# Half of an output projection computed as transposed fp32r products of split operands

## What is computed

```
y = y * rsqrt(mean(y*y, axis=-1) + 1e-6)      # 32 heads x 64 channels
y = y * silu(z)
attn = y.reshape(B, T, 2048) @ Wout.T         # (1024, 2048) x (2048, 256)
x = layernorm(x + attn)
```

## Time and profile before

| | |
|---|---|
| median of 3 runs | 721.79 us (719.56 to 722.85) |
| the profiled execution's own time | 723.31 us |
| span of its trace | 721.6 us |
| granted clock, mean over the span | 0.972 |
| PE busy | 658.7 us (91%) |
| PEld / DVE / POOL / ACT busy | 71% / 73% / 64% / 61% |

### The profile page before, as it was taken

One profiled execution on the slowest core, in us unless ns is written; L12 is line 12 of the kernel. 1 busy time (PEld: TensorE's weight loads), 2 busy tenths in 40 slices (PEclk: granted clock), 3 DMA queues, 4 the chain that ended last, 5 costly groups with the idle time before them and its releaser, 6 DMA issues.

```text
span 721.6 us, 11628 instructions
## 1 busy us (share of the span) xinstructions
PE 658.7 (91%) x3388; PEld 510.2 (71%) x3388; DVE 523.5 (73%) x848; ACT 437.3 (61%) x722; POOL 461.6 (64%) x440
## 2 busy tenths in 40 slices
PE   6689999999999999999999999899989998999920
PEld 3467777777777777777777777688867775677710
DVE  4879999999999999999999999613315574222236
ACT  3366797797797797797887887921014544333321
POOL 4066887987887987987888885840025648752034
PEclk9899999999999999999999999999999999999975
DMA  4311211211311211211211200371016914543124
GB/s 148 124 45 59 104 45 59 102 44 58 102 44 58 102 44 58 102 44 58 87 59 58 73 30 0 118 217 36 15 53 147 358 51 106 156 134 97 52 74 131
DMA packets 25475, 62.34 MB, mean 86 GB/s; under 512 B 5206, under 2 KB 18134, under 8 KB 22710
## 3 DMA queue, kind: packets, MB, share of 16 engines
q1 hardware_dynamic: 22278, 53.31, 21.8%
q0 software_dynamic: 3168, 8.67, 4.8%
HBM read 52.77 MB, written 9.20 MB: 86 GB/s over the span
## 4 chain that ended last, share of the span: by engine, by line
PE 83%; DVE 5%; POOL 4%; issue 3%; ACT 2%; DMA 2%; POOLq 0%; SPq 0%; DVEq 0%; ACTq 0%
PE ps L639 35%; PE ps L612 8%; PE ps L653 7%; PE ps L667 6%; PE ps L880 5%; PE ps L920 4%; PE ps L654 4%; DVE conv L1327 3%; POOL conv L577 2%; PE ps L624 2%; PE ps L676 1%; PE ps L768 1%; PE ps L898 1%; PE ps L790 1%; PE ps L872 1%
## 5 line engine op out<-in xcount | busy, mean ns | idle before, releaser
L1327 DVE SCALAR_TENSOR_TENSOR conv<-ps,w_raw,conv 128x506 f32<-128x506 f32 (+3 forms) x352 | 324.9, 935 | 19.9 <-ACT conv L1047 13.7
L639 PE MATMUL ps<-x_hi,w_hi 128*128 128x512 f32 x384 | 166.6, 434 | 9.9 <-DVE conv L1327 8.3
L1047 ACT ACTIVATE conv<-ps,w_raw 128x512 f32<-128x512 f32 x160 | 109.7, 686 | 100.9 <-PE ps L639 99.2
L639 PE MATMUL ps<-x_hi,w_lo 128*128 128x512 f32 x384 | 152.6, 397 | 0.0
L639 PE MATMUL ps<-x_lo,w_hi 128*128 128x512 f32 x384 | 151.9, 396 | 0.0
L404 POOL TENSOR_TENSOR decay<-cum_b,cum_tok 128x512 f32<-128x512 f32 (+1 forms) x128 | 103.2, 827 | 24.6 <-DVE cum_tok L1291 24.6
L639 PEld LDWEIGHTS ps<-x_hi,w_hi 128*128 128x128 f32 x384 | 73.4, 191 | 35.2 <-DVE conv L1327 20.4
L410 POOL TENSOR_TENSOR decay<-decay,mask 128x512 f32<-128x512 f32 x64 | 82.7, 1292 | 5.0
L639 PEld LDWEIGHTS ps<-x_hi,w_lo 128*128 128x128 f32 x384 | 73.0, 190 | 16.8
L639 PEld LDWEIGHTS ps<-x_lo,w_hi 128*128 128x128 f32 x384 | 73.7, 192 | 10.4
L653 PE MATMUL ps<-conv 128*128 128x256 f32 x256 | 78.1, 387 | 2.6 <-DVE xs L1302 1.9
(11 more groups left out here) (219 smaller groups left out, 991.7 us busy)
## 6 DMA issues: line engine op xcount, KB each, us to landing
cum_b<-cum_scratch SPq DMA_DIRECT2D x16, 1024.0 KB, 4.7
w_raw<-in_winT SPq DMA_DIRECT2D x16, 778.0 KB, 4.4
y_all<-in_wgu SPq DMA_DIRECT2D x4, 1408.0 KB, 19.2
ys_scratch<-y_blk SPq DMA_DIRECT2D x31, 128.0 KB, 1.8
late<-in_wdn SPq DMA_DIRECT2D x2, 1408.0 KB
x_scratch<-conv SPq DMA_DIRECT2D x19, 128.0 KB, 6.2
late<-in_woutT SPq DMA_DIRECT2D x1, 2048.0 KB, 8.2
res_scratch<-conv SPq DMA_DIRECT2D x11, 128.0 KB, 1.9
```

The costliest lines, as they stand in the source:

```text
L639: mm = pe.matmul(ps[:, j % 4, :], wp[:, par, w], xp[:, kk, t], start=(i == 0), stop=(i == 5))
L1047: act.activation(conv[:, par, tile, hf * 512:(hf + 1) * 512], ps[:, j % 4, :], ACT.Copy, scale=w_raw[:, par, tap:tap + 1]).then_inc(S["a_c ...
L1327: dve.scalar_tensor_tensor(out=o[:, :, s:], in0=u[:, :, 0:T - s], scalar=w_raw[:, par, c:c + 1], in1=o[:, :, s:], op0=ALU.mult, op1=ALU.ad ...
```

## The change

Blocks 4 to 7 (the last 512 tokens, `HALF`) are no longer computed by `out_project`. `project_half` computes them transposed: stationary is a 128 x 128 piece of the weight, moving are 512 tokens of one pair, the result is 128 outputs x 512 tokens, once for each half c of the 256 outputs (banks 4 and 5). Each product is made of three fp32r ones. So the weight and the half of `y_all` are split first: ACT copies the weight to `wo_hi` in four pieces and each pair to a ring of four buffers, `y_high`; the rests are subtracted by DVE (`wo_lo`, and `y_low` of pairs 0 to 3) and by POOL (`y_low` of pairs 4 to 15, in place of `y_all`). ACT copies the two results to `o_turned`, and PE turns them back with 8 transposes (`turn_half`, banks 6 and 7).

The order of the blocks in the normalization becomes 0, 1, 4, 5, 6, 7, 2, 3. Blocks 2 and 3 stay plain fp32 and come behind `project_half`. The buffers in the former space of `conv` are laid out anew; that moves the load of `ctx_w` and of half of `w_dn` on SP from ahead of the eight stores to behind the second of them, with a wait for the end of `project_half`.

```diff
+HALF = NT // 2
+YRING = 4
+ORDER = (0, 1, 4, 5, 6, 7, 2, 3)
...
@@ sync
-            sp.dma_start(ctx_w, ctxT.rearrange("e (k p) f -> p e k f", p=P)).then_inc(S["ld_ctx"], 16)
...
-            load_down(1)
-            for b in range(TB):
-                sp.wait_ge(S["n0"], b + 1)
+            for pos, b in enumerate(ORDER):
+                if pos == 2:
+                    sp.wait_ge(S["yh_done"], NPAIR)
+                    sp.dma_start(ctx_w, ctxT.rearrange("e (k p) f -> p e k f", p=P)).then_inc(S["ld_ctx"], 16)
+                    load_down(1)
+                sp.wait_ge(S["n0"], pos + 1)
...
@@ gpsimd
+            for i in range(YRING, NPAIR):
+                pool.wait_ge(S["a_yh"], i + 1)
+                t = slice(HALF, NT)
+                pool.tensor_tensor(y_low[:, i, t], y_all[:, i, t], y_high[:, i % YRING, :].bitcast(F32), ALU.subtract
+                                   ).then_inc(S["p_yl"], 1)
             pool.wait_ge(S["v_xin"], 1)
...
@@ tensor
+            def project_half():
+
+                for i in range(NPAIR):
+                    if i % 4 == 0:
+                        pe.wait_ge(S["v_wo"], i // 4 + 1)
+                    if i < YRING:
+                        pe.wait_ge(S["v_yl"], i + 1)
+                    else:
+                        pe.wait_ge(S["p_yl"], i + 1 - YRING)
+                    for c in range(KD):
+                        d = slice(c * P, (c + 1) * P)
+                        for k, (w, y) in enumerate(((wo_hi, y_high[:, i % YRING, :]), (wo_lo, y_high[:, i % YRING, :]),
+                                                    (wo_hi, y_low[:, i, HALF:NT]))):
+                            mm = pe.matmul(ps[:, 4 + c, :], w[:, i, d], y, start=(i == 0 and k == 0),
+                                           stop=(i == NPAIR - 1 and k == 2))
+                    mm.then_inc(S["yh_done"], 1)
+
+            def turn_half():
+
+                for c in range(KD):
+                    pe.wait_ge(S["a_oh"], c + 1)
+                for j in range(2):
+                    for b in (2 * j, 2 * j + 1):
+                        for c in range(KD):
+                            mm = pe.transpose(ps[:, 6 + j, (b % 2) * D + c * P:(b % 2) * D + (c + 1) * P],
+                                              o_turned[:, c, b * P:(b + 1) * P], ident[:, :])
+                    mm.then_inc(S["oh_done"], 1)
...
-            for b in range(TB):
-                if b >= 2:
-                    ge(pe, S["r0"], b - 1)
-                out_project(b, NPAIR - 1 if b < 2 else 0, NPAIR)
...
+            out_project(0, NPAIR - 1, NPAIR)
+            out_project(1, NPAIR - 1, NPAIR)
+            ranks_by_id()
+            project_half()
+            pe.wait_ge(S["r0"], 1)
+            out_project(2, 0, NPAIR // 2)
+            table_by_id()
+            turn_half()
+            out_project(2, NPAIR // 2, NPAIR)
+            pe.wait_ge(S["r0"], 2)
+            out_project(3, 0, NPAIR)
+            pe.wait_ge(S["r0"], 6)
...
@@ scalar
-            for b in range(TB):
-                layer_norm_scale(b, 0)
+            def high_y(i):
+
+                act.wait_ge(S["v_y"], 2 * i + 2)
+                if i >= YRING:
+                    act.wait_ge(S["yh_done"], i - YRING + 1)
+                act.activation(y_high[:, i % YRING, :], y_all[:, i, HALF:NT], ACT.Copy).then_inc(S["a_yh"], 1)
+
+            act.wait_ge(S["ld_wo"], 16)
+            for c in range(4):
+                part = slice(4 * c, 4 * c + 4)
+                act.activation(wo_hi[:, part, :], wo_sb[:, part, :], ACT.Copy).then_inc(S["a_wo"], 1)
+            for i in range(YRING):
+                high_y(i)
+            layer_norm_scale(0, 0)
+            layer_norm_scale(1, 0)
+            for i in range(YRING, NPAIR):
+                high_y(i)
+            act.wait_ge(S["yh_done"], NPAIR)
+            for c in range(KD):
+                act.activation(o_turned[:, c, :], ps[:, 4 + c, :], ACT.Copy).then_inc(S["a_oh"], 1)
+            for pos in range(2, TB):
+                layer_norm_scale(pos, 0)
...
@@ vector
             dve.wait_ge(S["ld_xt"], 16)
-            for b in range(TB):
-                ln_front(b, 0)
-                if b >= 1:
-                    ln_back(b - 1, 0, x1[:, b - 1, :])
...
+            owners_by_id()
+            for c in range(4):
+                dve.wait_ge(S["a_wo"], c + 1)
+                part = slice(4 * c, 4 * c + 4)
+                dve.tensor_tensor(wo_lo[:, part, :], wo_sb[:, part, :], wo_hi[:, part, :].bitcast(F32), ALU.subtract
+                                  ).then_inc(S["v_wo"], 1)
+            for i in range(YRING):
+                dve.wait_ge(S["a_yh"], i + 1)
+                t = slice(HALF, NT)
+                dve.tensor_tensor(y_low[:, i, t], y_all[:, i, t], y_high[:, i, :].bitcast(F32), ALU.subtract
+                                  ).then_inc(S["v_yl"], 1)
+            for n in range(TB):
+                ln_front(n, 0)
+                if n == 1 or n >= 3:
+                    ln_back(n - 1, 0, x1[:, ORDER[n - 1], :])
+                if n == 1:
+                    ln_back(1, 0, x1[:, ORDER[1], :])
                     slots_by_id()
                     tokens_by_id()
...
```

More of the change, by code:

```diff
@@ L83, in build_layer, with shadow @@
         w_raw = sb("w_raw", [P, 2, RAWW])
+        def shadow(name, shape, at):
+            return nc.alloc_sbuf_tensor_at(name, shape, F32R, offset=at)
+        conv_at = -(-nc.sbuf_base // 32) * 32
         conv = sb("conv", [P, 2, NCONV, NT])
@@ L86, in build_layer @@
         xs = sb("xs", [P, TB, P])
+        y_at = -(-nc.sbuf_base // 32) * 32
         y_all = sb("y_all", [P, NPAIR, NT])
@@ L111, in build_layer @@
                                               ("y_lo", [P, 512], F32R)))
+        late_at = -(-nc.sbuf_base // 32) * 32
         late = sb("late", [P, 2, NPAIR * D])
         wo_sb = late[:, 0, :].rearrange("p (i d) -> p i d", i=NPAIR)
+        wo_hi = shadow("wo_hi", [P, NPAIR, D], late_at + 4 * NPAIR * D)
+        wo_lo = shadow("wo_lo", [P, NPAIR, D], conv_at + 4 * YRING * HALF)
+        y_high = shadow("y_high", [P, YRING, HALF], conv_at)
+        y_low = shadow("y_low", [P, NPAIR, NT], y_at)
         xb = sb("xb", [P, NX, D])
@@ L132, in carve @@
             return conv_f[:, at[0] - n:at[0]]
+        xg = carve(TBS * D).rearrange("p (j d) -> p j d", j=TBS)
+        xgT, gT = (carve(2 * KD * P).rearrange("p (r k t) -> p r k t", r=2, k=KD) for _ in range(2))
+        slot_is = conv_f[:, at[0]:at[0] + PICKS * TBS * P // 2].bitcast(BF16).rearrange("p (k t) -> p k t", t=P)
+        ctx_w = carve(EX * KD * D).rearrange("p (e k f) -> p e k f", e=EX, k=KD)
+        at[0] = LATE = YRING * HALF + NPAIR * D
         x_tok = carve(TB * D).rearrange("p (b d) -> p b d", b=TB)
         x1 = carve(TB * D).rearrange("p (b d) -> p b d", b=TB)
[L135 to L142 removed]
+        x2T = conv_f[:, LATE:LATE + KD * TBS * P].rearrange("p (k t) -> p k t", k=KD)
+        res_tok = conv_f[:, LATE:LATE + TB * RES].rearrange("p (b r) -> p b r", b=TB)
+        y_of = conv_f[:, 0:PICKS * TB * D].rearrange("p (k b d) -> p k b d", k=PICKS, b=TB)
+        o_tok = conv_f[:, PICKS * TB * D:LATE].rearrange("p (b d) -> p b d", b=TB)
         g_tok = z_gate[:, 0, 0:2 * D].rearrange("p (r f) -> p r f", r=2)
@@ L183, in build_layer @@
         lane_p = take_c(1)
+        o_turned = take_c(KD * HALF).rearrange("p (c t) -> p c t", c=KD)
         step128 = take_c(TBS)
@@ L218, in build_layer @@
         ld_cum = [sem("ld_cum0"), sem("ld_cum1")]
-        ld_xb = [sem(f"ld_xb{i}") for i in range(NX)]
         st_y = [sem(f"st_y{i}") for i in range(NW)]
         ld_y = [sem(f"ld_y{b}") for b in range(TB)]
-        ld_xg = [sem(f"ld_xg{j}") for j in range(TBS)]
+        ld_row = [sem(f"ld_row{j}") for j in range(max(TBS, NX))]
         block = ctx.enter_context(nc.Block())
@@ L730, in _ @@
             out_project(1, 0, NPAIR - 1)
-            for b in range(TB):
-                if b >= 2:
-                    ge(pe, S["r0"], b - 1)
-                out_project(b, NPAIR - 1 if b < 2 else 0, NPAIR)
-                if b == 2:
-                    ranks_by_id()
-                if b == 6:
-                    table_by_id()
+            out_project(0, NPAIR - 1, NPAIR)
[10 more added lines that the diff above has]
+            pe.wait_ge(S["r0"], 6)
             for _ in range(11):
@@ L1367, in ln_front @@
                 if i == 0:
-                    dve.wait_ge(S["o0"], b + 1)
-                    dve.tensor_tensor(r, ps[:, b % 2, 0:D], x_tok[:, b, :], ALU.add).then_inc(S["r0"], 1)
+                    if 2 <= b < 6:
+                        dve.wait_ge(S["oh_done"], b // 2)
+                        src = ps[:, 5 + b // 2, (b % 2) * D:(b % 2 + 1) * D]
+                    else:
+                        dve.wait_ge(S["o0"], b + 1 if b < 2 else b - 3)
+                        src = ps[:, b % 2, 0:D]
+                    dve.tensor_tensor(r, src, x_tok[:, ORDER[b], :], ALU.add).then_inc(S["r0"], 1)
```

32 lines of the change are left out of this document (10 added, 22 removed).

## The result

| | before | changed |
|---|---|---|
| median | 722.75 us (12 runs) | 717.59 us (12 runs) |
| ratio to before | | 0.9937, 95% interval 0.9912 to 0.9962 |
| ratio, measured a second time | | 0.9948, 95% interval 0.9921 to 0.9976 |
| profiled execution, span | 723.31, 721.6 us | 716.46, 714.7 us |

The forecast was 719.8 us, a gain of 2.0. The kernel gained 4.5 and 3.8 us by the two ratios (0.63% and 0.52% of 722), just beyond the 0.5% that I had called indistinguishable from no change. The time lies in the range; the size of the gain was that of rival 1 (717.9 us), and it is larger than the -0.8 to -3.5 us that the prediction gave its own forecast.

A forecast was written before the change was run, and what follows sets the result against it. PE was taken to bound the kernel until the last block is ready. PE's -4.4 us, +1.1 stalls, +0.6 POOL and +0.8 loads, with small transitions, became -2.0: median 719.8 us, range 716.7 to 723.3.

The forecast's parts named there:

- rival 1: Splits hidden better: no loss to DVE's operations, loads land before the last store's issue, stall 0.5; 717.9 us, chance 0.27.
- The bound: PE alone bounds 494.58 to 529.5 us; moving "last block ready" moves the kernel's end one for one.
- The 96 products: On PE, the transposed half's fp32r products with 512 moving columns: 0.231 us each, 22.2 us together.
- The transposes: On PE, the 8 transposes that turn the half back: 1.0 us with the change of stage.
- The late splits: PE waits for splits: 0.2 us at pair 0, 0.9 at pair 4; +1.1 us together, bounds 0.3 and 2.
- POOL slowed by DVE, +0.6: `slots_by_id` on DVE lengthens POOL's subtractions: two times 0.44 us less two pairs' spare time; bounds 0 and 2.5.
- The loads ahead of the stores, +0.8: On SP's queue, stores of positions 2 to 7 stand behind `ctx_w` and half of `w_dn`; bounds 0 and 5.3 us.
- reckoning by places: Times added along PE from pair 4 to the last block, ready at 526.4 us against 529.5.
- the two allowances for contention: +0.6 us for POOL slowed by DVE's `slots_by_id`, +0.8 us for stores waiting behind loads on SP.
- Rival 2: POOL sets the pace: twelve subtractions at 1.69 us, the half 3.6 us above PE's need; 722.8 us, chance 0.13.
- Rival 3: On SP's queue from 511 us, stores wait for the load of `w_dn`: 2.1 us slower, 723.9 us, chance 0.15.
- Rival 4: Granted clock at 1.2 GHz between 576 and 578 us, behind a PE pause: 1 us either way; no chance given.

The follow-up runs named there:

- fp32_turned: Against the changed kernel, the transposed half is 32 plain fp32 products without any splits or waits for them; median 720.35 us, ratio to before 0.9989.
- split_early: Against the changed kernel, ACT's four copies to `wo_hi` stand ahead of its last root of the mixer; median 716.0 us, ratio to before 0.9926.
- slots_late: Against the changed kernel, DVE begins `slots_by_id` only when POOL's twelve subtractions are done; median 718.0 us, ratio to before 0.9953.
- tables_2: Against the changed kernel, two more DVE operations of comparison-table size stand ahead of `slots_by_id`; one run of 714.65 us, no ratio.
- loads_at_7: Against the changed kernel, the loads of `ctx_w` and `w_dn` are issued behind the seventh store instead of the second; median 733.79 us, ratio to before 1.0194.
- tables_6: Against the changed kernel, six more DVE operations of comparison-table size stand ahead of `slots_by_id`; median 719.47 us, ratio to before 0.9966.
- after_third: The changed kernel once more, unchanged, for one more profile; one run of 717.41 us.
- after_13: The changed kernel with 13 instead of 11 matmuls that nobody reads, ahead of the first gathered rows; 716.96 us, ratio to before 0.9941.

## Why the forecast came out as it did

- **The bound.** Right. The last block came 3.67 us sooner, and store, gather and sort followed at the old distance (10.2 us in both, 10.45 in one profile of the kernel before). The stretch moved the end one for one.
- **The 96 products.** Mis-sized by little: 0.2338 us each instead of 0.231, 22.44 instead of 22.2. The orientation is worth 0.16 us (fp32_turned).
- **The transposes.** 514.62 - 513.72 = 0.90 against 1.0.
- **The late splits.** Right in mechanism and nearly in size. At the start 0.5 against 0.2 (the products start 15.15 us after the first product of `out_project`, 14.64 in fp32_turned, which waits for no split); at pair 4, 0.70 against 0.9. Together 1.2 against 1.1, and split_early took them away for 1.3.
- **POOL slowed by DVE, +0.6.** The term that failed by its place, not by its kind. I had allowed POOL the spare time of two pairs. But `slots_by_id` starts with short operations, and its two long ones came at 499.40, 7.6 us after POOL's first start, and lengthened its eighth and ninth subtractions. Seven pairs had gone by: 7 x (1.394 - 1.254) = 0.98 us of lead. POOL lost 0.94 us in all (slots_late) and PE nothing; put at the front, two such operations cost 0.5 (tables_2). The short operations, for which my upper bound had 1.6 us, cost POOL nearly nothing: it was DVE that waited. Five of them lasted 1.21 to 1.29 us, where they take 0.16 to 0.34 alone, and nobody waited for DVE. The Trainium skill, "SBUF — State Buffer", section "Who interferes with whom", says that the two lock each other out; DVE's rows agree with it (L1499: 0.16 us in slots_late, 1.21 beside POOL), POOL's by less: 0.45 us for an operation of 0.69 us alone.
- **The loads ahead of the stores, +0.8.** It measured 0. The range of 0 to 5.3 was fair, since loads_at_7 shows what a store pays for loads ahead of it. Of my two landing times, 529.6 and 527, the second was still late: the loads were over by about 525.5, and the last store was issued at 527.40. By the second time, which lies ahead of my issue time of 528.6, the term is 0. Loads some 2 us longer would have held up the last store.
- **A wait that went away, -0.3.** Not in the sum: block 2 no longer stands behind block 1 and so no longer waits for DVE's first reading. The prediction's reckoning by places does hold it, since it ends at 526.4, 3.1 us ahead of 529.5, where the sum without the 0.8 of the loads gives 2.7; I didn't notice that the two differ.
- **The sum.** -27.71 + 22.44 + 0.90 + 0.51 + 0.70 - 0.32 = -3.48; the two plain blocks that remain take 0.18 less, which makes -3.66, and the stretch measured -3.67. Without the two terms that measured 0, the forecast's sum had -4.4 + 1.1 = -3.3: every part of it but the two allowances for contention was within 0.3 us. That it came so near the measured 3.67 is in part luck, since it lacked two gains of 0.3 and 0.2.
- **Rivals and chances.** Rival 1 came true in its time and in two of its three conditions: no loss to DVE's operations, and the loads landed in time. Its stall of 0.5 measured 1.2; the two gains that no sum had made up for most of that. Rival 2 (POOL paces) needs many long operations of DVE, and early; tables_6, with six more at the front, lost 1.7 of its 3.6. Rival 3 didn't happen, by its margin. Rival 4 is why single spans mislead: a fall was worth 1 to 5 us, not 1, and came in the kernel before and in variants of the changed one; and the pause of 0.55 us ahead of the one at 576 us was released by POOL (L518); I had put it down to a table load, for which the trace gives no wait of PE. I gave 0.68 to "within 0.5%" and 0.23 to "faster by more". Both ratios lie just beyond the line, so the less likely one came, though their intervals reach to both sides of it.

## What to carry to other kernels

When a helper engine is a little faster than the engine that it feeds, its lead grows with every step; a disturbance is paid only as far as it exceeds the lead at the time it comes. So cost a contention by when it falls, not only by how long it is, and put an engine's long conflicting work late in such a stretch. And measure a small edit by the time between two marks around it, which repeats to some hundredths, rather than by whole spans, which moved by up to 4.5 us here for reasons that lay elsewhere.

## What was not expected of the hardware

Much of the spread of this kernel's time goes with the granted clock. Beside the falls behind the sort there is one at the start, in code that no edit touches, behind a pause of PE of 1.10 to 1.13 us that all fourteen profiles share. The stretch behind that pause, first of after_third, then of tables_2:

```profile
44.00:46.00 2.00, 2.00 (x7) 1.52 (x6) 0.00 (x0) 0.00 (x0) 1.92 (x3) 0.50 0.86 327
```

```profile
42.00:44.00 2.00, 2.00 (x11) 1.64 (x10) 0.23 (x1) 1.02 (x2) 1.92 (x3) 1.00 0.82 321
```

The four profiles without this fall (split_early, tables_2, after_13, fp32_turned) reach `out_project` at 469.4 to 470.6 us, all the others at 471.3 to 473.1. Two executions with the same pauses can be granted different clocks, and what decides it these runs don't show.

A store of 128 KB that was issued right behind 2.4 MB of loads on the same engine's queue landed after 14.4 us against 1.7 (loads_at_7). And where DVE and POOL work on SBUF together, DVE bears most of it: its operations of 0.2 us last until POOL's of 1.25 is over, while POOL's gets longer only by DVE's long ones.
